# Attention row sums: four key blocks joined by three accumulating DMAs and two summing passes, with the value products cut in eighths of 64 columns

## The reference, cut to what matters

```python
qkv = einsum('bnd,ed->bne', x, w_qkv)
dots = einsum('bhnd,bhmd->bhnm', q, k) * SCALE
attn = softmax(dots, axis=-1)
out = einsum('bhnm,bhmd->bhnd', attn, v)
```

## Time and profile before

| what | value |
|---|---|
| median of 3 runs | 1830.68 us (1829.48 to 1830.99) |
| span of the profiled execution | 1825.5 us |
| PE busy | 1787.7 us, 98% of the span |
| DVE busy | 1455.1 us, 80% |
| ACT busy | 1448.1 us, 79% |
| POOL busy | 182.8 us, 10% |
| accumulating DMAs | 64 of 1 MB, median 8.0 us from issue to landing |

### The profile page before, as it was taken

The page is one execution under the profiler, slowest core; times in us unless marked ns, Lnnn a source line. Parts: engine busy times, 40 slices in busy tenths (PEclk is TensorE's granted clock), DMA queues, the critical chain, the costliest instruction groups (busy, mean ns, idle before and its releaser), DMA issues. The chain is left out here.

```text
span 1825.5 us, 40458 instructions
## 1 busy us (share of the span) xinstructions
PE 1787.7 (98%) x16186; PEld 906.5 (50%) x16186; DVE 1455.1 (80%) x1582; ACT 1448.1 (79%) x1581; POOL 182.8 (10%) x158
## 2 busy tenths in 40 slices
PE   9999998999999999999999999999989999999997
PEld 7887885333333333333333333333336776644443
DVE  5444346889899898898998989989984778788898
ACT  5344357999999999999999999999965555556487
POOL 0000000010010010010010010100113221000044
PEclk9999999999999999999999999999999999999998
DMA  8665555436446346355464463464456440122075
GB/s 300 216 226 205 206 201 180 105 87 166 96 99 170 93 101 166 82 134 133 94 142 124 94 164 91 108 160 96 102 140 215 139 138 24 64 127 127 1 295 206
DMA packets 106370, 256.32 MB, mean 140 GB/s; under 512 B 8180, under 2 KB 24692, under 8 KB 96756
## 3 DMA queue, kind: packets, MB, share of 16 engines
q1 hardware_dynamic: 97012, 187.08, 28.5%
q0 software_dynamic: 9216, 67.11, 19.8%
HBM read 105.01 MB, written 82.05 MB: 102 GB/s over the span
## 5 line engine op out<-in xcount | busy, mean ns | idle before, releaser
L896 DVE TENSOR_TENSOR dve_sum<-dve_sum,probs 128x2048 f32<-128x2048 f32 x320 | 737.8, 2306 | 13.1 <-ACT probs L817 3.3
L817 ACT ACTIVATE probs<-score_others,shift_now 128x1536 f32<-128x1536 f32 x384 | 597.5, 1556 | 0.0
L984 PE MATMUL mixed_ps<-probs,value_piece 128*32 128x512 f32 (+1 forms) x3840 | 407.9, 515 | 1.2 <-ACT probs L817 0.2
L816 ACT ACTIVATE probs<-score_first,shift_now 128x512 f32<-128x512 f32 x384 | 266.5, 694 | 4.1 <-PE score_others L951 1.1
L951 PE MATMUL score_first<-first_queries,key_piece 32*128 32x512 f32 x768 | 245.4, 424 | 4.6 <-ACT probs L816 3.0
L951 PE MATMUL score_others<-first_queries,key_piece 32*128 32x512 f32 x2304 | 247.8, 425 | 0.0
L951 PE MATMUL score_others<-q_second,key_piece 32*128 32x512 f32 x2304 | 247.3, 424 | 0.0
L951 PE MATMUL score_first<-q_second,key_piece 32*128 32x512 f32 x768 | 245.1, 424 | 0.1
L951 PEld LDWEIGHTS score_first<-q_second,key_piece 32*128 32x128 f32 x768 | 122.0, 183 | 183.6 <-ACT probs L816 100.8
L951 PEld LDWEIGHTS score_first<-first_queries,key_piece 32*128 32x128 f32 x768 | 121.8, 183 | 183.2 <-ACT probs L816 84.3
L817 ACT ACTIVATE probs_paired<-score_others,shift_now 128x1536 f32<-128x1536 f32 x128 | 198.2, 1548 | 0.0
(11 more groups left out here) (252 smaller groups left out, 2596.7 us busy)
## 6 DMA issues: line engine op xcount, KB each, us to landing
probs_paired<-probs_paired POOLq DMA_DIRECT2D x64, 1024.0 KB, 8.0
o_scratch<-out_parts SPq DMA_DIRECT2D x33, 512.0 KB, 2.8
k_scratch<-parts SPq DMA_DIRECT2D x32, 512.0 KB, 4.9
q_scratch<-parts SPq DMA_DIRECT2D x32, 512.0 KB, 2.7
key_piece<-k_scratch SPq DMA_DIRECT2D x32, 512.0 KB, 5.2
h_scratch<-h SPq DMA_DIRECT2D x5, 2816.0 KB, 8.1
h<-h_scratch SPq DMA_DIRECT2D x5, 2816.0 KB, 11.4
v_scratch<-values SPq DMA_DIRECT2D x32, 256.0 KB, 2.0
```

Of the source, the lines that this page charges most:

```text
L816: nc.scalar.activation(block_probs(k)[:, 0:CH], score_first[:], ACT.Exp, bias=shift[:, c:c + 1], scale=SCALE).then_inc(probs_done, 1)
L817: nc.scalar.activation(block_probs(k)[:, CH:HPG * CH], score_others[n % 2][:], ACT.Exp, bias=shift[:, c:c + 1], scale=SCALE).then_inc(prob ...
L896: nc.vector.tensor_tensor(total[:], first[:], block_probs(k)[:], ALU.add).then_inc(dve_added, 1)
L984: last = nc.tensor.matmul(mixed_ps[j * HD:(j + 1) * HD, lo:hi], v_group[k // KPP][:, k % KPP, j * HD:(j + 1) * HD], block_probs(k)[:, j * ...
```

## The change

It changes four things in `attend`.

1. The paired blocks are (2, 3) and (4, 5). Each pair is joined as before by a DMA, but POOL issues it when PE has used the pair's first block for the values and ACT has written the second one. When both have landed (`pair_joined`), POOL issues a third DMA that adds the first pair's sum into the second pair's (L929 of the changed kernel), and it lands in `four_joined`.
2. PE sums two tiles and not three: the sum of four blocks in step 0, `dve_sum` in step 1.
3. The value work is counted in eighths of 64 columns: none in steps 0 and 1, 9 eighths in steps 2 to 13, 10 in steps 14 and 15.
4. The waits follow: ACT writes block 2 when `four_landed` tells that the third DMA of the chunk before is there, blocks 3 and 5 when `pairs_landed` tells it of the pairs, block 4 when the sums are done. DVE still adds twelve blocks in 11 additions, now 0, 1 and 6 to 15.

```diff
-    PAIRS = ((4, 5), (9, 10))
-    TO_SUMS = (0, 1)
+    PAIRS = ((2, 3), (4, 5))
-    SUMS_AT = ((0,), (1, 2))
+    SUM_PARTS = 2
+    SUMS_AT = ((0,), (1,))
-    VALUE_HALVES = (0, 0, 2, 2, 3, 2, 2, 3, 2, 2, 3, 2, 2, 3, 2, 2)
-    HALF = CH // 2
+    VALUE_PARTS = (0, 0, 9, 9, 9, 9, 9, 9, 9, 9, 9, 9, 9, 9, 10, 10)
+    PARTS = 8
+    PART = CH // PARTS
@@ scalar
-                            if i in TO_SUMS:
+                            if i is not None and k == PAIRS[i][1]:
+                                act.wait_ge(pairs_landed, it * CPB + c + 1)
+                            elif i == 0:
+                                act.wait_ge(four_landed, it * CPB + c + 1)
+                            elif i == 1:
                                 act.wait_ge(sums_done, it * CPB + c + 2)
@@ gpsimd
-                            pool.wait_ge(mixed_done, (it + 1) * BLOCKS + c * KB + pair[1] + 1)
+                            pool.wait_ge(mixed_done, (it + 1) * BLOCKS + c * KB + pair[0] + 1)
+                            pool.wait_ge(probs_done, (it + 1) * EXPS + (c * KB + pair[1] + 1) * 2)
                             pool.sem_inc(may_join, 1)
-                            nc.gpsimd.dma_start(probs_paired[i][0][:], probs_paired[i][1][:], accum_op=ALU.add).then_inc(joined[i], 16)
+                            nc.gpsimd.dma_start(probs_paired[i][0][:], probs_paired[i][1][:], accum_op=ALU.add).then_inc(pair_joined, 16)
+                        pool.wait_ge(pair_joined, 16 * len(PAIRS) * (it * CPB + c + 1))
+                        pool.sem_inc(pairs_landed, 1)
+                        nc.gpsimd.dma_start(probs_paired[1][0][:], probs_paired[0][0][:], accum_op=ALU.add).then_inc(four_joined, 16)
...
+                        pool.wait_ge(four_joined, 16 * (it * CPB + c + 1))
+                        pool.sem_inc(four_landed, 1)
@@ tensor, sums(f, at)
-                    if at < len(TO_SUMS):
-                        part = probs_paired[TO_SUMS[at]][0]
-                        pe.wait_ge(joined[TO_SUMS[at]], 16 * f)
+                    if at == 0:
+                        part = probs_paired[1][0]
+                        pe.wait_ge(four_joined, 16 * f)
```

More of the change, by code:

```diff
@@ L698, in attend @@
         dve_added, may_join = sem("dve_added"), sem("may_join")
-        joined = [sem(f"joined{i}") for i in range(len(PAIRS))]
+        pair_joined, four_joined = sem("pair_joined"), sem("four_joined")
+        pairs_landed, four_landed = sem("pairs_landed"), sem("four_landed")
         mixed_copied = sem("mixed_copied")
@@ L884, in _ @@
                             k = ADD_ORDER[a + 1]
[L885 to L888, removed]
+                            v.wait_ge(probs_done, (it + 1) * EXPS + (c * KB + k + 1) * 2)
                             if a == 0:
@@ L927, in _ @@
                             nc.gpsimd.tensor_tensor(w_flat[1][:, now], w_raw[:, now], w_flat[0][:, now].bitcast(F32), ALU.subtract).then_inc(w_lo_done, 1)
-                for signal in joined:
-                    pool.wait_ge(signal, 16 * ITERS * CPB)
+                        pool.wait_ge(four_joined, 16 * (it * CPB + c + 1))
+                        pool.sem_inc(four_landed, 1)
             @block.tensor
@@ L971, in sums, with values @@
                         last = nc.tensor.matmul(mixed_ps[j * HD:(j + 1) * HD, :], keep.ones[:, 0:HD], part[:, j * CH:(j + 1) * CH],
-                                                start=at == 0, stop=at == len(TO_SUMS))
-                    if at == len(TO_SUMS):
+                                                start=at == 0, stop=at == SUM_PARTS - 1)
+                    if at == SUM_PARTS - 1:
                         last.then_inc(sums_done, 1)
-                def values(f, k, halves):
+                def values(f, k, parts):
                     pe.wait_ge(probs_done, EXPS + (f * KB + k + 1) * 2)
@@ L981, in values @@
                         pe.wait_ge(sums_read, 1 + f + 1)
-                    lo, hi = halves[0] * HALF, (halves[-1] + 1) * HALF
+                    lo, hi = parts[0] * PART, (parts[-1] + 1) * PART
                     for j in range(HPG):
@@ L985, in values @@
                                                 block_probs(k)[:, j * CH + lo:j * CH + hi], start=k == 0, stop=k == KB - 1)
-                    if halves[-1] == 1:
+                    if parts[-1] == PARTS - 1:
                         last.then_inc(mixed_done, 1)
@@ L1000, in _ @@
                     done = 0
-                    for step, halves in enumerate(VALUE_HALVES):
+                    for step, parts in enumerate(VALUE_PARTS):
                         if f * KB + step + AHEAD < CHUNKS * KB:
@@ L1006, in _ @@
                         for k in range(KB):
-                            now = [half for half in range(2) if done <= 2 * k + half < done + halves]
+                            now = [part for part in range(PARTS) if done <= PARTS * k + part < done + parts]
                             if now:
                                 values(f, k, now)
-                        done += halves
+                        done += parts
                 def first_product(t):
@@ L1015, in first_product @@
                                          start=m == 0, stop=m == len(terms) - 1)
-                for at in range(len(TO_SUMS) + 1):
+                for at in range(SUM_PARTS):
                     sums(CHUNKS, at)
```

3 lines of the change are left out of this document (1 added, 2 removed).

## The result

The changed kernel takes 1866.55 us at the median of 4 runs (1864.33 to 1868.44), the kernel before on the same chip 1830.84 (1829.48 to 1831.94): a ratio of 1.019, with an interval of 1.0173 to 1.0207. It is slower by 1.9%; forecast were 0.9% faster.

The account below looks back on a forecast made before the run. PE was taken as the bound: 32.11 + 0.30 + 0.07 = 32.48 us a chunk against 33.15; with small waits -0.65 x 31 = -20.2, plus 4 for loads, -16.2: median 1814.5 us, range 1806 to 1829.

Parts of the forecast that it names:

- One sum less, step 1, the wait for DVE: PE, each chunk: one sum less saves 0.853 us; after step 1's score PE waits 0.30 for DVE's last addition.
- DVE's margin of 0.3 before its copy: DVE, each chunk: additions end at T + 32.3, values are free for the copy at T + 32.6, so covered.
- Rival 3: DVE becomes the bound, by slower additions or a later copy: period 32.6 to 32.9, 1819 to 1828 us; chance 0.10.
- Narrow pieces at 0: PE's three 64-column value pieces a chunk cost nothing extra; the upper end was 0.34 us a chunk.
- rival 1: PE's narrow 64-column waves cost 0.11 us each: 10.6 us more in all, 1825 us; chance 0.12.
- Even value steps, -0.1: PE's value steps in eighths keep PE and ACT in step, removing waits from uneven steps: -0.1 us a chunk.
- Three DMAs in a chain, quiet chunks: POOL's chain in chunks c < 3: third DMA lands at T + 30.5 to 31.6, hidden by 2 us or more, cost 0.
- The same chain beside SP's loads: POOL's chain in chunks c = 3: third DMA lands about T + 34, 0.6 us late, 7 places, 4 us taken.
- the case of 2.1 us more: Chunks c = 3: if SP's piece 2 also gets ahead of the third DMA, it lands 2.1 us later.
- The upper price: Upper end of the chain's cost beside SP's loads: 2.5 us in each of 7 places, 18 us in all.
- The stage's end, 0: End of the stage: it waits for the same last addition of DVE, so no time was gained or lost there.
- Rival 2: Chunks c = 3: queues share the DMA engines, third DMA lands at T + 37.5, 4.1 late; 1837 us; chance 0.10.

Follow-up runs that it names:

- the filler: The changed kernel with five float32 products of 512 columns before PE's wait for the third DMA, in eight places; 1855.15 us, ratio 1.0129.
- the first experiment: The changed kernel with SP issuing pieces 1 and 2 of the next keys and values only after block 12 of chunk 3; 1858.96 us, ratio 1.016.

## Why the prediction was wrong

The sum for the stage failed in the landing of the DMA chain and in what a wait for it costs. In the order of its steps:

- *One sum less, step 1, the wait for DVE.* Right. Quiet periods were forecast at 32.50 and are 32.46 to 32.94. Those 22 of them without a late DMA have a mean of 32.61, where 0.02 was allowed for small waits and it takes 0.13: 2.5 us in all. The wait for DVE's last addition is 0.2, near the 0.3 forecast, and DVE's margin of 0.3 before its copy held. (Rival 3's time is 1 us high by its own numbers: 31 x 0.1 to 31 x 0.4 over 1814.5 is 1818 to 1827.)
- *Narrow pieces at 0.* Right: the kernel before in eighths is 0.02 a period faster, not 0.34 slower, so rival 1 is out. *Even value steps, -0.1:* mostly wrong, 0.02 in the kernel before, and nothing in the chain's kernel (32.48 to 32.8 in halves).
- *Three DMAs in a chain, quiet chunks.* The size was off. "Hidden, by 2 us or more" (by its own numbers 33.4 less 31.6, 1.8) took the second pair's landing at T + 23.0 and the third at T + 31.6 at the latest; where T itself isn't behind a wait they land at T + 23.2 to 25.1 and T + 31.5 to 34.1, in chunk 10 at T + 35.3. The step that failed: it took 6.9 us for the first DMA, the fastest of the 64, before adding 5.6 for the second. With the median of 8.0 that gives T + 24.1, and T + 32.7 for the third, 0.7 before it is needed. The margin was thin in every chunk; in two of the 24 quiet ones it went, and two periods took 34.1: 3.2 us.
- *The same chain beside SP's loads.* This is the step that made the prediction wrong. "0.6 late", 4 us taken in 7 places, with 2.5 each as the upper end. It lands at T + 38.0 and not T + 34, 4.6 late; in the seven chunks it is T + 37.5 to 40.4. The forecast had counted the bytes of piece 0, 2.1 us, and had the second pair at T + 25.1. It lands at T + 28.0: the DMA next to the loads took 13.1 us from issue to landing, its bulk was moved by T + 26.3, and its last packets came 1.4 us after that. The third DMA then had this late pair ahead of it and more loads than were counted: piece 2 was issued at T + 26.4, and its keys got ahead too, which the forecast had as the case of 2.1 us more and did not take. The run with all loads behind the pairs takes the cause away and gets T + 33.5.
- *A wait of PE costs more than its length.* The sum had no term for it. After 4.0 to 5.5 us without work PE ran at the lower clock for 3.4 to 5.3 us: 1.3 to 2.5 us more at each of seven places, as the filler shows. The upper price was 2.5 each (17.5 us) for all of it; the seven cost 40.9 more than before.
- *The stage's end, 0.* Wrong. I left out that chunk 31 runs the same chain beside the next stage's first loads (L615); the chain is T + 38.6 there and costs 6.7 us.

Put together: 1010.9 us were forecast from T of chunk 0 to T of chunk 31 (1027.1 less 16.2), 1059.2 are measured, 48.3 more. Against 32.50 a period and the 4 us for the loads, 42.0 of them are in the seven periods and 5.7 in the other 24; the rest is that a period before is 33.13 by PE's T and not 33.15. With 6.7 at the end and 1.0 at the start that is the 55.9 by which the span exceeds 1809.3. The median stood 1.4 above this span and not 5.2.

Rival 2 had the landings nearly right, T + 28.5 and T + 37.5, and 4.1 us late, from transfers that share the engines. It had a chance of 0.10 and a price of 1837: the clock and the stage's end are what it lacked. Its mechanism is not what the rows show. While the second pair moved, SP had a store waiting, issued at 416.46, and of 415 to 420 POOL's queue has almost all; in 421 to 423 it is the other way:

```profile
q0 software_dynamic: 121, 0.97, 93.8%
q1 hardware_dynamic: 177, 0.14, 9.5%
...
q1 hardware_dynamic: 745, 0.73, 103.3%
q0 software_dynamic: 2, 0.01, 2.0%
```

Transfers go nearly in order of arrival, as the prediction said, but the end of one overlaps the start of the next: from 421 to 423 two packets of POOL's DMA are left, and its landing at 422.7 waits for them. The forecast's arithmetic of bytes has no such term. The Trainium skill's DMA: Bandwidth & Descriptors (section Queues, rings and completion order) describes each engine as switching between the queues packet by packet; the shares of these windows don't show that for POOL's and SP's queues.

Why the last packets lag can be read from the traces. Each of these DMAs ends with 16 packets of 4 bytes, which I take to be one for each engine. Often 15 of them come close together and one later, and then a packet of the queue of kind `instruction` stands in the time of the DMA; these packets have 16 KB each (1.92 MB in 117 on the page before). The clearest case is in the kernel before, the first DMA of chunk 1, which has no load or store beside it and landed 9.1 us after its issue. Fifteen engines are done by 351.84; the window 352.34:353.31 holds only this:

```profile
q8 instruction: 1, 0.02, 6.1%
q0 software_dynamic: 1, 0.00, 0.2%
```

The packet of 16 KB takes one engine of 16 from 352.34 to 353.30, and the DMA's last packet comes right behind it. The same holds throughout: of the 992 DMAs in the eleven traces, 245 had no such packet in their time or that of the DMA still under way before them, and in 244 of these the last engine was done less than 0.4 us after the fifteenth; of the 747 with one, 505 had one engine 0.4 to 2.5 us behind. In quiet chunks too the second pair has such a tail, 0.5 to 1.7 us from the median engine to the last; it uses up most of the margin that the forecast saw there. The trace doesn't number the engines; that the instruction packet and the late ones share an engine is read from their times, and no run was made that moves these packets. The loads beside the chain shift the bulk: in chunk 3 half of the engines are done with the second pair at T + 25.6, in quiet chunks at T + 22.3. Of these 3.3 us, 2.1 are piece 0 as counted, and 1.2 are that the first pair, with SP's first packets beside its end, is done at T + 18.5 and not at T + 17.3.

The Trainium skill's TensorE: Matmul & The Clock Gate (section HAM oscillation — how this bites in real kernels) has a kernel that waits for a DMA, again and again, restart each time on the slow clock. The 0.51 in 432.80 to 436.30 agrees, and it was in reach of the prediction, had it asked what follows a wait of 4 us.

## What to carry to other kernels

When work goes from an engine to a chain of DMAs, add up the chain from the median landing and not from the fastest one, and once more beside every load that the kernel issues in that time, at the ends of the stage too; the margin of 0.7 us in 33 that the median would have given here was none. Ask what the waiting engine pays on top of the wait. And if the chain is late, the cheapest cure here was to start it earlier, by giving the consumer of its inputs those blocks first: 4 us earlier gave back the whole gain, 1815 us against 1867.

## What the runs showed of the hardware

- A DMA of 1 MB that adds one SBUF tile into another moved in 5.5 us of all 16 engines (28.2% x 1865.2 / 96) and, as the first of its chunk in the kernel before (and in its variant in eighths), with no load or store beside it, landed after 6.9 to 7.0 us in the 14 cases without a packet of the queue of kind `instruction` in its time and after 7.0 to 9.2 us in the 34 with one. With 0.79 MB of loads between it and the one ahead it landed after 13.0 us (chunk 3 of the first experiment), the last 2 of them at a share of 0.05.
- A load issued 0.1 us after POOL's DMA (T + 27.4 and T + 27.3, end of the stage) moved ahead of it.
- TensorE's waits of 4.0 to 5.5 us came with 3.4 or 6.8 us at 1.2 GHz, 3.4 to 5.3 of them in its work; two waits of 1.8 and 1.9 us did not, three of 2.1 to 2.9 us in the run with all loads behind both pairs did (3.4 us each). With five float32 products by ones in the wait's place it stayed at 2.4 GHz, which was worth 1.3 to 2.5 us a place.
- Value products in pieces of 64 columns cost nothing that could be seen beyond their columns: with 3 narrow pieces in a chunk and even steps the period was 0.02 us shorter.
